# Transposes of a head's probabilities in larger groups

## What is computed

```python
x  = L0_attn_x                        # 1024 tokens x 512
xn = layernorm(x)
q  = rmsnorm(xn @ Wq.T, q_norm_w)     # 32 heads of 128
k  = rmsnorm(xn @ Wk.T, k_norm_w)     # 8 groups of 128, 4 heads share one
v  = xn @ Wv.T
scores = q @ k.T / sqrt(128) + slope * (key - query)   # later keys: -1e30
o  = softmax(scores) @ v
s  = o @ Wo.T
g  = silu((silu(xn @ gate) * (xn @ up)) @ down)        # 4-bit weights, expanded
out = x + s * g
```

## Time and profile before

| | |
|---|---|
| median of 3 runs | 1333.64 us (1332.92 to 1333.79) |
| the profiled execution | 1337.71 us, its span 1335.5 us |
| TensorE busy, share of the span | 1284.6 us, 96% |
| VectorE busy | 976.8 us, 73% |
| ScalarE busy | 649.4 us, 49% |
| GpSimd busy | 751.5 us, 56% |
| transposes of probabilities (L845) | 1152, 191.8 us busy |

### The profile page before, as it was taken

How to read it: one execution, slowest core, us unless ns; L and a number is a source line. 1 busy time by engine, 2 the same in 40 slices (tenths; PEclk the granted TensorE clock), 3 DMA queues, 4 the chain that set the end, 5 groups by cost and what they waited for, 6 DMA issues and landing times. The chain is left out here.

```text
span 1335.5 us, 20919 instructions
## 1 busy us (share of the span) xinstructions
PE 1284.6 (96%) x7120; PEld 1103.6 (83%) x7120; DVE 976.8 (73%) x2067; ACT 649.4 (49%) x1420; POOL 751.5 (56%) x730
## 2 busy tenths in 40 slices
PE   5799999999999999999999999999999989999996
PEld 5688888888888888888888888888888878888884
DVE  5677787787778777877787778777888844555556
ACT  2555555556555555555555555555555523222222
POOL 3745575557555655565566556555565625555553
PEclk9799999999999999999999999999999999999998
DMA  3000000010000000100010000000020035444431
GB/s 120 16 17 17 33 16 17 17 32 17 16 17 32 17 17 16 33 16 17 17 32 17 17 17 33 17 17 16 17 70 18 1 112 160 134 129 130 129 104 63
DMA packets 29467, 57.87 MB, mean 43 GB/s; under 512 B 3648, under 2 KB 3648, under 8 KB 29248
## 3 DMA queue, kind: packets, MB, share of 16 engines
q1 hardware_dynamic: 29376, 56.68, 14.5%
HBM read 54.57 MB, written 2.10 MB: 42 GB/s over the span
## 5 line engine op out<-in xcount | busy, mean ns | idle before, releaser
L390 POOL TENSOR_TENSOR pb<-rel,coef 128x1024 f32<-128x1024 f32 (+7 forms) x256 | 298.3, 1183 | 94.9 <-PE T L845 89.9
L479 ACT ACTIVATE pb<-pb,low 128x1024 f32<-128x1024 f32 (+7 forms) x256 | 198.8, 777 | 188.0 <-DVE low L652 186.9
L469 ACT ACTIVATE pt_h<-T 128x512 fp32r<-128x512 f32 (+3 forms) x384 | 185.8, 486 | 123.1 <-PE T L845 119.9
L636 DVE TENSOR_TENSOR pt_l<-T,pt_h 128x512 fp32r<-128x512 f32 (+3 forms) x384 | 210.1, 549 | 43.2 <-ACT pt_h L469 41.9
L652 DVE CUSTOM_DVE_ANT_0 pb<-S,pb,ninv 128x1024 f32<-128x1024 f32 (+7 forms) x256 | 207.4, 810 | 38.3 <-PE S L867 33.2
L845 PE MATMUL T<-ident,pb 128*128 128x128 f32 x1152 | 191.8, 276 | 19.4 <-DVE pb L661 13.0
L845 PEld LDWEIGHTS T<-ident,pb 128*128 128x128 f32 x1152 | 142.3, 142 | 60.1 <-DVE pb L661 20.4
L661 DVE TENSOR_SCALAR pb<-pb,rinv 128x1024 f32<-128x1024 f32 (+7 forms) x256 | 170.6, 666 | 9.0
L864 PE MATMUL S<-kT_h,q_h 128*128 128x512 f32 (+2 forms) x384 | 142.8, 372 | 2.7 <-DVE kT_l L724 2.7
L368 POOL TENSOR_TENSOR root<-ms,cst 128x4 f32<-128x4 f32 x64 | 76.3, 1193 | 117.1 <-DVE ms L684 117.1
L883 PE MATMUL O<-pt_h,v_h 128*128 128x512 f32 (+2 forms) x384 | 140.7, 366 | 1.0 <-DVE pt_l L636 1.0
(11 more groups left out here) (138 smaller groups left out, 2931.4 us busy)
## 6 DMA issues: line engine op xcount, KB each, us to landing
wq_in<-in_wq SPq DMA_DIRECT2D x32, 256.0 KB, 2.8
wo_in<-in_wo SPq DMA_DIRECT2D x32, 256.0 KB, 2.6
stage<-in_wkv SPq DMA_DIRECT2D x8, 512.0 KB, 4.2
stage<-in_gate_w SPq DMA_DIRECT2D x14, 256.0 KB, 2.6
stage<-in_gate_z SPq DMA_DIRECT2D x14, 256.0 KB, 3.5
stage<-in_gate_s SPq DMA_DIRECT2D x14, 256.0 KB, 4.9
stage<-in_up_w SPq DMA_DIRECT2D x14, 256.0 KB, 5.3
stage<-in_up_z SPq DMA_DIRECT2D x14, 256.0 KB, 6.2
```

The costliest lines, as they stand in the source:

```text
L390: g_.tensor_tensor(pbuf(idx, t), rel[:, TOK - w:TOK], coef[:, t:t + 1].to_broadcast([P, w]), ALU.mult).then_inc(bias_ready, 1)
L469: a_.activation(pt_lot(pt_h, t, n), bank[:, 0:m * P].rearrange("p (k w) -> p k w", w=P), ACT.Copy).then_inc(tr_hi, 1)
L479: a_.activation(pbuf(idx, t), pbuf(idx, t), ACT.Exp, bias=low[:, idx:idx + 1], scale=-1.0, accum_out=rsum[:, idx:idx + 1]).then_inc(exps_r ...
L636: v_.tensor_tensor(pt_lot(pt_l, t, n), bank[:, 0:m * P].rearrange("p (k w) -> p k w", w=P), f(pt_lot(pt_h, t, n)), ALU.subtract).then_inc( ...
```

## The change

No instruction is added or removed. Each of these is made of whole lots that change their place, on TensorE and, to match, on ACT and DVE:

- (6,0) moves behind unit 1 and stands beside (6,1).
- (5,0) and (5,1) stand together after the 8th matmul of q_proj qc1 (before: ahead of it and after its 6th).
- (4,0) moves behind unit 2 and stands beside (4,1).
- Tiles 3 and 2 stand together after the 5th matmul of values v1 (before: ahead of it and after its 12th).
- Tiles 1 and 0 of the head before stand together after the 6th matmul of q_proj qc0 (before, tile 1 stood ahead of it).
- On DVE q_lo comes ahead of logits 4, and lots 5 and 4 follow normalise 3 and normalise 4; on ACT the two lots of tile 5 follow exp 3, and those of tile 4 follow exp 4.
- In the last head unit 2 comes ahead of tile 5.

With ss0, ss1 and tile 7, TensorE goes from matmuls to transposes at 8 places in a head; before it was at 13.

```diff
@@ ScalarE
-                lot(h, 5, 0)
                 exp(h, 3)
-                lot(h, 5, 1)
+                lots(h, 5)
                 if more:
                     q_hi(at, f"qc1_{(j + 1) % PER}")
-                lot(h, 4, 0)
                 exp(h, 4)
-                lot(h, 4, 1)
+                lots(h, 4)
                 exp(h, 5)
@@ VectorE
                 normalise(h, 2)
-                lot(h, 6, 0)
                 if w:
                     project(at, f"w1_{j}", unit + 1)
-                lot(h, 6, 1)
+                lots(h, 6)
                 logits(h, 3)
-                lot(h, 5, 0)
                 normalise(h, 3)
-                lot(h, 5, 1)
-                logits(h, 4)
+                if not more:
+                    project(at, f"w2_{j}", unit + 2)
+                lots(h, 5)
                 if more:
                     q_lo(at, f"qc1_{nx}")
-                else:
-                    project(at, f"w2_{j}", unit + 2)
-                lot(h, 4, 0)
+                logits(h, 4)
                 normalise(h, 4)
                 if w and more:
                     project(at, f"w2_{j}", unit + 2)
-                lot(h, 4, 1)
+                lots(h, 4)
                 logits(h, 5)
@@ TensorE
-                if prev:
+
+                def head_before(h=h):
                     lots(h - 1, 1)
+                    lots(h - 1, 0)
+
                 if j > 0:
-                    q_proj(at, f"qc0_{j}", h, {6: [lambda h=h: lots(h - 1, 0), lambda h=h: scores(h, 1)]})
+                    q_proj(at, f"qc0_{j}", h, {6: [head_before, lambda h=h: scores(h, 1)]})
                 elif prev:
-                    q_proj(at, f"qc0_{j}", h, {6: [lambda h=h: lots(h - 1, 0)]})
+                    q_proj(at, f"qc0_{j}", h, {6: [head_before]})
...
                 w_unit(0)
-                lot(h, 6, 0)
                 w_unit(1)
-                lot(h, 6, 1)
+                lots(h, 6)
                 scores(h, 3)
-                lot(h, 5, 0)
                 if more:
-                    q_proj(at, f"qc1_{nx}", h + 1, {6: [lambda h=h: lot(h, 5, 1)]})
+                    q_proj(at, f"qc1_{nx}", h + 1, {8: [lambda h=h: lots(h, 5)]})
                 else:
                     w_unit(2)
-                    lot(h, 5, 1)
+                    lots(h, 5)
                 scores(h, 4)
-                lot(h, 4, 0)
                 if more:
                     w_unit(2)
-                lot(h, 4, 1)
+                lots(h, 4)
                 scores(h, 5)
...
                 scores(h, 6)
-                lots(h, 3)
-                values(at, f"v1_{j}", h, g + 1 if j == 0 else None, {12: [lambda h=h: lots(h, 2)]})
+
+                def two_lots(h=h):
+                    lots(h, 3)
+                    lots(h, 2)
+
+                values(at, f"v1_{j}", h, g + 1 if j == 0 else None, {5: [two_lots]})
```

## The result

The changed kernel takes 1379.13 us (1377.48 to 1381.00, 4 runs), the kernel before 1333.72 us (1332.92 to 1335.13, 4 runs): ratio 1.0336, 95% interval 1.0322 to 1.0350. The forecast was 1375 us in a range of 1358 to 1388. The profiled executions took 1378.97 us (span 1376.8) and 1337.71 us (span 1335.5); between their spans lie 41.3 us, where the sum of the prediction had 41.4.

What follows compares the result with a forecast made beforehand. TensorE's own work was taken as the bound. Terms 29.4 + 1.6 + 6.6 + 1.0 + 3.6 - 0.8 = 41.4 us on the profiled 1337.7 gave 1379.1, less 4.1: 1375 us, range 1358 to 1388.

Steps and rivals of the forecast that it cites:

- squares1, groups 0 to 6: In kv_proj, TensorE waits for DVE's read of (4,0): 29.4 us in 28 heads, 1.6 us in heads 0 and 1.
- ss0 behind POOL's lock: POOL's bias slows tile 7's multiplication, ss0 is read 0.15 us later in 24 heads: 3.6 us.
- last group: squares1 waits 2.48 us in each of 3 heads, tile 2 waits 0.9, pt_l waits go: 6.6 us together.
- last head: Tile 4's lots straight behind scores 4, values waiting for the same chain: 1.0 us, between 0 and 3.
- places: Moving between matmuls and transposes at 160 fewer places gains 0 to 1.6 us, taken as 0.8.
- each step of the chain: From ACT's square through q_lo, logits 4, exp 4, normalise 4 and unit 2's addition, (4,0) is read at 521.61; TensorE arrives 520.74.
- Tile 2's 0.9 us: In the last group, ss1 is read about 0.3 us after TensorE reaches tile 2: 0.9 us more.
- Edits at nothing: Moves of tiles 6, 5, 3 and 2 and POOL's later biases were taken to cost nothing.
- the thinnest cover, tile 2's: DVE's sum for ss1 ends 0.2 us before tile 2 wants its bank; each 0.1 beyond costs 2.8 us.
- tile 5: Its transposes arrive at 514.5 and its banks were read at 513.5, so no cost was expected.
- the median of the runs is 4.1 us below that execution: Last step, from the profiled execution's 1379.1 us to the forecast median of 1375 us.

Runs made afterwards that it cites:

- experiment 7: Kernel before with squares1, tile 3 and tile 2 transposes put singly among matmuls, 244 more places: 1338.57 us, ratio 1.0020.
- experiment 12: Changed kernel with logits 4 first and normalise 4 last on DVE, POOL waiting for tile 7's multiplication, squares0 earlier, last group's squares1, tiles 3 and 2 later: 1333.66 us.
- experiment 1: Changed kernel with squares1 after the 21st of kv_proj's 24 matmuls and not the 12th: 1364.02 us, ratio 1.0216.
- experiment 2: Changed kernel with (4,0) and (4,1) back in their old places on all three engines, 9 places: 1346.66 us, ratio 1.0078.
- experiment 3: Changed kernel with only DVE's order altered, unit 2's addition and lots 4 ahead of normalise 4: 1359.39 us, ratio 1.0174.
- experiment 4: As experiment 3, with logits 4 also ahead of q_lo on DVE, still 8 places: 1343.04 us, ratio 1.0062.
- Experiment 6: As experiment 4, with POOL's bias for idx 2 waiting for DVE's multiplication of tile 7 where j > 0: 1339.08 us, ratio 1.0027.
- experiment 5: As experiment 4, with tile 1 of the head before again ahead of q_proj qc0 on TensorE, 9 places: 1342.39 us, ratio 1.0054.
- experiment 9: Kernel before with squares0 after v0's 7th matmul and POOL's idx 0 bias of a group's first head waiting for tile 0's multiplication: 1343.14 us, ratio 1.0051.

## Why the prediction was right

Where the 41.3 us between the two profiled spans went, from start to start on TensorE in the two traces (the places at the 0.006 us of experiments 7 and 12):

| term | predicted | measured |
|---|---|---|
| squares1, groups 0 to 6 | 31.0 | 30.8 |
| ss0 behind POOL's lock | 3.6 | 3.7 |
| last group | 6.6 | 10.3 |
| last head | 1.0 | 1.8 |
| places | -0.8 | -1.0 |
| waits that went in heads 1, 2 and 30 | 0 | -3.1 |
| ahead of every moved lot | 0 | -1.0 |
| sum | 41.4 | 41.5 |

The last term is none of the change's: at the first transposes of squares, at 38 us, where both kernels have done the same work, the changed one is already 1.0 us ahead.

- **squares1**: right in size and in each step of the chain. Experiments 1 to 4 show the cause: each version that has DVE read tile 4 sooner, or TensorE come to squares1 later, loses that much of the wait.
- **ss0 and POOL**: right, though its price was a remainder of small margins. Experiment 6 shows it.
- **The last group** is the term that was mis-sized. squares1 waits 2.44 us in each of its 3 heads (predicted 2.48). But behind each the clock is half for 3.4 us, which costs 1.7 us, 5.1 in all; the step took work after a wait at its usual price, and none of the rows in front has a wait as long as that. The trace of the kernel before does have one, in its first head (TensorE's row behind the wait, then a window):

```profile
42.67 0.50 PE L864 MATMUL S<-kT_h,q_h 128*128 128x512 f32 x1 [2.67 <-DVE kT_l L724]
```

```profile
43.00:47.00 4.00, 4.00 (x13) 3.26 (x12) 1.75 (x3) 0.57 (x2) 4.00 (x4) 0.57 0.00 0
```

  So the toll could have been read ahead of the change. Tile 2's 0.9 us does not show, since a slowed TensorE arrives late. Less the waits that went, 2.1 us, this is 7.3 + 5.1 - 2.1 = 10.3. Experiment 3 gives the other side: its squares1 waits in the last group were 1.74 us, and no half clock followed.
- **The last head**: 1.8 within the 0 to 3 given.
- **Places**: right. Experiment 7 measures 0.005 us each in its trace and 0.011 (0.004 to 0.018) in its times.
- **Tile 0**, a gain that the prediction lacked. In the kernel before TensorE waits for tile 0 of the head before in heads 1 and 2 (0.6 us each) and 30 (1.4), and for another lot in head 1 (0.5). Around the longest of these, timelines of DVE, POOL and TensorE, and last the DVE row of the same work in the changed kernel:

```profile
1018.33 3.21 DVE L797 TENSOR_TENSOR stage<-stage 128x512 f32<-128x512 int32 x2
1021.47 0.15 DVE L658 RECIPROCAL rinv<-rsum 128x1 f32<-128x1 f32 x1
...
1019.53 1.47 POOL L390 TENSOR_TENSOR pb<-rel,coef 128x768 f32<-128x768 f32 x1 [0.41 <-PE T L845]
...
1022.00 0.33 PE L845 MATMUL T<-ident,pb 128*128 128x128 f32 x1 [1.22 <-DVE pb L661]
...
1055.42 1.29 DVE L792 TENSOR_TENSOR stage<-stage 128x512 f32<-128x512 int32 x2
```

  Two subtractions on DVE run beside POOL's bias and take 3.21 us, not 1.29; the reciprocal of tile 0 is late, and TensorE stands. Tile 1's move takes that bias out of the way. Experiments 4 and 5 differ in tile 1's place alone: with it back, tile 0's waits are there in the same three heads. In head 30 the bias then meets tile 0's own multiplication (1.35 us for 0.29) and not the subtractions, so of the 1.4 us only 0.5 come back.
- **"Edits at nothing"**: the thinnest cover, tile 2's, held in the changed kernel only because squares1's pause protected it (experiment 1). For tile 5 only the banks that it needs were looked at, not when it is read for tile 4 behind it; unit 2 between them covers that in the changed kernel, and where unit 2 stands behind (4,0) the cover is gone (experiment 2).
- **The step that was off** is "the median of the runs is 4.1 us below that execution". The profiled execution, at 1337.71, was within the ordinary spread: 15 further runs of the kernel before lay at 1332.03 to 1338.31 us, median 1336.28, so it was the median of three that lay low. The changed kernel's profiled execution lies 0.15 us from its median. Without the subtraction the forecast is 1379.1, and the median came at 1379.13; with the 1.4 us that the 15 runs allow it is 1377.7. That close a hit is partly luck: the 4.5 us by which the last group and the last head were too small stand against 4.3 us that nobody forecast, the waits that went, the lead at 38 us and 0.2 of the places. The ratio of 1.0336 rests on four low runs of the kernel before; against 1336.28 the changed kernel is 42.9 us slower, a ratio of 1.032.

## What to carry to other kernels

Before lots are put together, follow what each engine has ahead of them in its queue: here 160 places fewer saved about 1 us in all, and two moves on DVE cost 1.03 us a head: normalise 4, which waits for another engine, put ahead of the reading of the bank (0.71, experiment 3), and q_lo put ahead of logits 4 (the other 0.32, experiment 4). A stall protects the covers behind it, so one repaired wait can uncover a second (experiment 1), and a contended operation pushed later looks for another victim (experiment 9): check the next two meetings of the same two engines before a wait is added. Compare a profiled execution with the other kernel's profiled execution, and take no offset from a median of three runs.

## What the runs showed of the hardware

- TensorE's granted clock was at half for 3.4 us behind all three waits of 2.28 us in the last group of the changed kernel (and all three in experiment 1), and behind four of the six waits of 2.05 us in experiment 9. Behind the idle times of 0.9 to 1.8 us in the changed kernel and in experiment 3, from 60 us on, it stayed full. The toll, 1.7 us, is nearly as large as the wait.
- A DVE multiplication that meets a POOL tensor operation took 1.43 us for 0.75 (changed kernel), 2.33 for 0.75 (experiment 9), 1.36 for 0.29. In these three it ended 0.55, 0.55 and 0.08 us behind the end of POOL's operation, which is 0.2 us less than its own length. Two DVE subtractions of 128x512 took 3.21 us for 1.29 beside a bias of 1.47.
- Going from matmuls to transposes and back costs 0.005 to 0.006 us by the traces (experiments 7 and 12), 0.011 by the times (0.004 to 0.018).
- The runs of the kernel before go with the mean granted clock: those at 0.995 lie at 1332.0 to 1334.4 us, those at 0.990 to 0.992 at 1335.7 to 1338.9. Differences of medians under 2 us are thus not resolved here.
